# Causal attention with a rotated relative term: the query's rotation taken from its own product by four VectorE passes and moved a quarter of a step forward, and stage-start loads regrouped

## What is computed

```python
def _attn(xn, Wq, bq, Wk, bk, Wv, bv, Wo, bo, u):
    q = xn @ Wq.T + bq ; k = xn @ Wk.T + bk ; v = xn @ Wv.T + bv   # split into 16 heads of 8
    ...
    scores = q @ k.transpose
    rel = (q + u) @ r.transpose          # r: sin/cos position rows
    scores = (scores + _rel_shift(rel, S, S)) * HEAD_DIM ** (-0.5)
    ...                                   # causal mask, softmax, times v, out projection
```

## Time and profile before

| | us |
|---|---|
| median of three executions | 6445.04 |
| lowest, highest | 6442.2, 6449.46 |
| profiled execution | 6442.88 |
| its span | 6441.2 |
| granted TensorE clock, mean | 0.946 |
| busy: PE, DVE, ACT, POOL | 88%, 65%, 44%, 32% |

### The profile page before, as it was taken

One profiled execution on the slowest core, in us unless ns is written; L12 is line 12 of the kernel. 1 busy time (PEld: TensorE's weight loads), 2 busy tenths in 40 slices (PEclk: granted clock), 3 DMA queues, 4 the chain that ended last, 5 costly groups with the idle time before them and its releaser, 6 DMA issues. The chain is left out here.

```text
span 6441.2 us, 121160 instructions
## 1 busy us (share of the span) xinstructions
PE 5668.1 (88%) x38029; PEld 3515.6 (55%) x38029; DVE 4211.3 (65%) x9620; ACT 2847.4 (44%) x4602; POOL 2039.8 (32%) x2936
## 2 busy tenths in 40 slices
PE   8996999999996999879987998889988989875677
PEld 5663444444443777457754776467754556533464
DVE  6884666666664787367844786368745656577764
ACT  4553222222221555435553555445544645433344
POOL 6551000000002665156623665156620012251012
PEclk9998999999997999989998999899999999987799
DMA  4332332333334554055512554055510000000002
GB/s 132 108 104 89 97 97 96 99 95 96 96 98 108 145 150 127 6 135 149 149 49 74 147 149 112 7 154 151 150 27 4 0 3 0 5 4 0 0 2 60
DMA packets 526325, 526.98 MB, mean 82 GB/s; under 512 B 55698, under 2 KB 436705, under 8 KB 503780
## 3 DMA queue, kind: packets, MB, share of 16 engines
q1 hardware_dynamic: 517684, 517.90, 29.0%
q10 hardware_dynamic: 8320, 5.25, 0.3%
HBM read 337.88 MB, written 185.07 MB: 81 GB/s over the span
## 5 line engine op out<-in xcount | busy, mean ns | idle before, releaser
L351 DVE TENSOR_REDUCE a_mx<-a_unit 128x2 f32<-128x512 f32 (+1 forms) x1920 | 1295.1, 685 | 522.7 <-PE a_unit L537 506.6
L441 ACT ACTIVATE a_prob<-a_slot 128x1536 f32<-128x1536 f32 x640 | 929.1, 1452 | 575.6 <-PE a_slot L560 452.0
L535 PE MATMUL a_unit<-a_sk,a_sq 96*128 96x256 bf16 (+3 forms) x5120 | 758.7, 251 | 173.8 <-DMA a_sk<-a_kscratch 152.4
L1126 ACT ACTIVATE f_silu<-f_pG 128x512 f32<-128x512 f32 x528 | 315.0, 598 | 933.1 <-PE f_pG L1199 919.0
L537 PE MATMUL a_unit<-a_maskq,identb 128*128 128x256 bf16 (+1 forms) x1920 | 605.8, 316 | 0.0
L535 PEld LDWEIGHTS a_unit<-a_sk,a_sq 96*128 96x128 bf16 (+1 forms) x5120 | 373.0, 99 | 412.3 <-issue 168.5
L1068 DVE TENSOR_TENSOR f_gated<-f_spread,f_silu 128x512 f32<-128x512 f32 x512 | 354.6, 693 | 347.1 <-ACT f_silu L1126 307.0
L1178 PE MATMUL f_pO<-f_hidden,f_wd 128*128 128x512 f32 x1056 | 545.0, 598 | 13.5 <-DVE f_hidden L1070 13.3
L1199 PE MATMUL f_pG<-f_xnT,f_wg 128*128 128x512 f32 x1056 | 541.5, 594 | 0.0
L1203 PE MATMUL f_pU<-f_xnT,f_wu 128*128 128x512 f32 x1056 | 540.1, 593 | 0.0
L60 POOL TENSOR_SCALAR f_veps<-f_moments 128x4 f32<-128x4 f32 (+1 forms) x112 | 25.4, 227 | 1493.3 <-DVE f_moments L955 1031.0
(11 more groups left out here) (397 smaller groups left out, 11079.4 us busy)
## 6 DMA issues: line engine op xcount, KB each, us to landing
f_spread<-f_scratch SPq DMA_DIRECT2D x1024, 128.0 KB, 2.9
a_sq<-a_qscratch SPq DMA_DIRECT2D x128, 768.0 KB, 5.7
a_sk<-a_kscratch SPq DMA_DIRECT2D x160, 384.0 KB, 6.6
a_qscratch<-a_parts SPq DMA_DIRECT2D x288, 192.0 KB, 2.3
a_qscratch<-a_parts SPq DMA_DIRECT2D x288, 128.0 KB, 2.2
a_kscratch<-a_parts SPq DMA_DIRECT2D x160, 192.0 KB, 2.2
a_kscratch<-a_parts SPq DMA_DIRECT2D x160, 128.0 KB, 2.1
a_qscratch<-a_parts SPq DMA_DIRECT2D x288, 64.0 KB, 1.9
```

The costliest lines, as they stand in the source:

```text
L351: v.tensor_reduce(dst, src, op=ALU.max, axis=AX.X, negate=True).then_inc(red_done, 1)
L441: act.activation(prob[gr % 2][:, :], slot[:, :], ACT.Exp, scale=SCALE).then_inc(exp_done, 1)
L535: pe.matmul(bank[:, at * wide:(at + 1) * wide], q, sk[b][0:KM, gr * GH + h, 0:wide], start=(at == 0), stop=False)
L1126: act.activation(silu[c % 2][:, :], pG[c % 2][:, :], ACT.Silu).then_inc(silu_done, 1)
```

## The change

In `attention`:

- The weights `u12`, their load, the second product (L652) and its semaphore go. DVE forms `u1` and `u2` from the query/key product's own result, in which a head's features lie in another order, by four passes over 64 partitions each (`rotated`), from the halves of `ring[1]`'s query part and a rearranged table `turn`. Two passes come after the reduction of unit 4, two after that of unit 5; before, two passes of 128 partitions came after unit 7.
- DVE: the normalisation moves from after unit 4 to after unit 8, the division from after unit 5 to after unit 6.
- PE: the transposes of the normalised rows move to right behind scores(0), the query/key product to behind maxima(2), the value-projection product of n+1 comes after maxima(7), where that of n came after maxima(0).
- ACT: the copy-out of the transposed rows and the query/key product move ahead; the copy of the value projection follows the third group's exponentials, for n+1.
- POOL: `causal(2)` moves from ahead of the splitting chain to between the first subtraction and the second cast.

In the feed-forwards of the group and of l2: the weights, statistics and the first normalised tile live in a `FeedHead` that outlives the attention; the attention loads the weights, and in its last two steps makes the statistics of blocks 0 and 1 and normalises block 0. The performer only loads the weights. Nothing but PE and ACT waits for the weights, ACT runs one Gelu ahead, and g2's gain has a semaphore of its own, for which POOL waits a block later.

In `routed_experts`: the router's three arrays load first, on a semaphore of their own, for which DVE and PE wait; PE waits for the expert weights at its first expert product; ACT runs one Sigmoid ahead and doesn't wait.

```diff
@@ attention, POOL
                     causal(1)
-                    causal(2)
...
                         chain.link(g.tensor_copy(pt[:, :, 0, :], f32s[:, :, :]))
                         chain.link(g.tensor_tensor(rest[:, :, :], f32s[:, :, :], pt[:, :, 0, :], op=ALU.subtract))
+                    causal(2)
+                    if is_seq(n + 4):
+                        pt = parts[j % 2]
                         chain.link(g.tensor_copy(pt[:, :, 1, :], rest[:, :, :]))
...
+                    if head is not None and isinstance(n, int) and n >= SEQS - 1:
+                        blk = n - SEQS + 1
+                        g.wait_ge(head.stats_done, blk + 1)
+                        ln_rstd(g, chain, head.moments, head.veps, head.mhalf, head.rstd, eps, head.rstd_done, apart)
@@ attention, DVE
                     units(3, 5)
+                    def rotated(c, u):
+                        low = slice(c * D // 2, (c + 1) * D // 2)
+                        for o in range(2):
+                            ins = v.scalar_tensor_tensor(out=u[o * D // 2:(o + 1) * D // 2, :], in0=ring[1][low, 0:SEQ],
+                                                         scalar=b12s[low, c:c + 1], in1=turn[low, o, :],
+                                                         op0=ALU.add, op1=ALU.mult)
+                        return ins
...
+                    if rel and is_seq(n + 4):
+                        v.wait_ge(qk_taken, n + 5)
+                        if is_seq(n + 3):
+                            v.wait_ge(u_added, n + 4)
+                        rotated(0, u1)
                     units(5, 6)
+                    if rel and is_seq(n + 4):
+                        rotated(1, u2).then_inc(u_taken, 1)
+                    units(6, 7)
...
-                        v.scalar_tensor_tensor(out=u1[:, :], in0=ring[1][:, 0:SEQ], scalar=b12s[:, 0:1],
-                                               in1=turn[:, 0, :], op0=ALU.add, op1=ALU.mult)
-                        v.scalar_tensor_tensor(out=u2[:, :], in0=ring[1][:, SEQ:2 * SEQ], scalar=b12s[:, 1:2],
-                                               in1=turn[:, 1, :], op0=ALU.add, op1=ALU.mult).then_inc(u_taken, 1)
@@ attention, PE
                     scores(0)
-                    maxima(0)
-                    (value-projection product of n)
+                    (transposes of the normalised rows of n+4)
+                    maxima(0)
                     values(n - 1, (j + 1) % 2, 3)
                     maxima(1)
                     maxima(2)
+                    (query/key product of n+4)
...
                     maxima(7)
-                    if rel and is_seq(n + 4):
-                        pe.wait_ge(qk_taken, n + 5)
-                        for c in range(2):
-                            ins = pe.matmul(ring[1][:, c * SEQ:(c + 1) * SEQ], u12[:, c * D:(c + 1) * D], xnT[j % 4][:, :],
+                    if is_seq(n + 1):
+                        if is_seq(n + 4):
+                            pe.wait_ge(u_taken if rel else qk_taken, n + 5)
+                        (value-projection product of n+1)
@@ attention, DVE, end of the step
+                    if head is not None and once(n, SEQS - 1):
+                        v.drain()
+                        ln_stats(v, chain, rows(store, 0, BT), head.stats, head.moments, head.stats_done)
+                    if head is not None and once(n, SEQS):
+                        v.wait_ge(head.rstd_done, 1)
+                        ln_apply(v, rows(store, 0, BT), head.moments, head.rstd, head.xn).then_inc(head.xn_done, 1)
+                        v.drain()
+                        ln_stats(v, chain, rows(store, BT, BT), head.stats, head.moments, head.stats_done)
@@ feed_forward
             @block.gpsimd
-                g.wait_ge(w_in, W_IN)
+                    if gb is not None and once(n, 1):
+                        g.wait_ge(gain_in, 16)
             @block.scalar
-                act.wait_ge(w_in, W_IN)
+                act.activation(warm[:, :], core["ident"][:, 0:1], ACT.Gelu)
+                act.wait_ge(w_in, head.W_IN)
@@ routed_experts
+                for dst, src in ((wr[:, :], w["router"]), (bias[:, 0, :], w["bias"].partition_broadcast(P)),
+                                 (tri[:, :], core["tri"].partition_broadcast(P))):
+                    sp.dma_start(dst, src).then_inc(router_in, 16)
             @block.vector
-                v.wait_ge(w_in, W_IN)
+                v.wait_ge(router_in, ROUTER_IN)
             @block.tensor
-                pe.wait_ge(w_in, W_IN)
+                pe.wait_ge(router_in, ROUTER_IN)
...
+                        if once(n, 0):
+                            pe.wait_ge(w_in, W_IN)
```

More of the change, by code:

```diff
@@ L156, with attention @@
 KPART = [0, 1, 2, 0, 1, 0]
-def attention(nc, core, tag, store, eps, w, kept, layer=None, arriving=None):
+def attention(nc, core, tag, store, eps, w, kept, layer=None, arriving=None, head=None, head_w=None):
     rel = kept.rel
@@ L245, in _ @@
                     arriving.others(sp)
+                if head is not None:
+                    head.load(sp, head_w, layer)
                 def step(i, j):
@@ L493, in step @@
                     exps(2)
+                    if once(n, -1):
+                        act.wait_ge(kept.filled, 1)
+                    if is_seq(n + 1):
+                        act.wait_ge(v_pe, n + 2)
+                        if is_seq(n - 1):
+                            act.wait_ge(pv_done, n * GROUPS)
+                        hot = vaug[(j + 1) % 2][:, :, :, :].rearrange("p t (r f j) e -> p (t r) f j e", f=2, j=GH)
+                        got = ring[1][:, 0:SEQ].rearrange("p (a f j e) -> p a f j e", f=2, j=GH, e=HD)
+                        for f in range(2):
+                            ins = act.activation(hot[:, :, f, :, 16 * f:16 * f + HD], got[:, :, f, :, :], ACT.Copy)
+                        ins.then_inc(v_taken, 1)
                     if is_seq(n - 1):
@@ L589, in step @@
                     scores(0)
-                    maxima(0)
-                    if is_seq(n):
-                        if is_seq(n + 3):
-                            pe.wait_ge(u_taken if rel else qk_taken, n + 4)
-                        elif is_seq(n - 1):
-                            pe.wait_ge(v_taken, n)
-                        xb = xnT[j % 4]
-                        for t in range(QT):
-                            ins = pe.matmul(ring[1][:, t * D:(t + 1) * D], xb[:, t * P:(t + 1) * P], wq[:, 2 * D:3 * D],
-                                            start=True, stop=True)
-                        ins.then_inc(v_pe, 1)
-                    values(n - 1, (j + 1) % 2, 3)
-                    maxima(1)
                     if is_seq(n + 4):
@@ L611, in step @@
                         ins.then_inc(t_pe, 1)
+                    maxima(0)
+                    values(n - 1, (j + 1) % 2, 3)
+                    maxima(1)
                     maxima(2)
+                    if is_seq(n + 4):
+                        if once(n, -4):
+                            pe.wait_ge(w_qk, W_QK)
+                        pe.wait_ge(xnT_done, n + 5)
+                        for c in range(2):
+                            ins = pe.matmul(ring[1][:, c * SEQ:(c + 1) * SEQ], wq[:, c * D:(c + 1) * D], xnT[j % 4][:, :],
+                                            start=True, stop=True)
+                        ins.then_inc(qk_pe, 1)
                     if is_seq(n + 1):
@@ L742, in step @@
                 def step(n, b):
+                    if isinstance(n, int) and n < head.begun:
+                        return
                     if within(n + 2):
@@ L833, in _ @@
                 deep(pe, step)
+        for s in head.held.sems:
+            nc.gpsimd.sem_clear(s)
         k.clear()
@@ L1519, in _ @@
                     sp.dma_start(omega[h * HD:(h + 1) * HD, h * M:(h + 1) * M], w["omega"]).then_inc(w_in, 16)
+                head.load(sp, head_w)
             @block.gpsimd
```

152 lines of the change are left out of this document (75 added, 77 removed).

## The result

| | before | changed |
|---|---|---|
| median, us | 6446.61 (4 runs, 6442.2 to 6449.46) | 6563.24 (4 runs, 6553.9 to 6574.52) |
| profiled span | 6441.2 | 6562.3 |
| granted clock, mean | 0.946 | 0.945 |
| busy: PE, DVE, ACT, POOL | 88, 65, 44, 32% | 86, 66, 43, 31% |

The ratio of the runs is 1.0182, with a 95% interval of 1.0165 to 1.02: the change costs 117 us. The forecast was slower by 55 us (6500, range 6425 to 6600). The direction and the mechanism held; the size came out at twice the forecast, and one term of the sum carries most of that.

The account below looks back on a forecast made before the run. PE, busy 88%, was taken to bound the kernel, waiting mainly for the read-back of the split keys. The terms 52 − 8 − 2 + 44 − 15 − 13 − 4 − 2 = +52 gave 6500 us, range 6425 to 6600.

Parts of the forecast that it names:

- the stage starts: Earlier loads and statistics at the feed-forward and router stages: f0 −15, f1 −13, and −4 for a gain awaited late.
- a0: The first attention, without a rotation, its step set by DVE and PE together: −2 us, bounds −6 and +3.
- the steady step: Relative attention: rotation ends at 9.3 to 9.4, select at 14.5, step 16.6 us against 16.1; +52 us over 26 × 4.
- The clock: PE's granted clock falls behind the new wait on POOL's select in one step of four: +44 us.
- the clock holds: Rival: no clock falls behind PE's new wait in the attentions, so 6456 us; chance 0.13.
- a fall in every step: Rival: PE's clock falls behind the new wait in each of 104 steps, +177, so 6633 us; chance 0.08.
- The ramps: The ramp in at the start of the relative attention layers: −2 us, bounds −8 and +8.
- The last steps: A layer's last steps, without rotation, save the product and have no new wait: about 2 us a layer, −8.
- f0: Routed-experts stage: with the router's small arrays loaded first, DVE's first pass starts at 546 instead of 560.72: −15 us.
- f1: The layer group's feed-forward: loads made during attention remove a 3.6 us wait, less 0.3 for a table load; −13 in four layers.
- the rotation arrives in time: Rival: rotation done by about 7.2 us, select ready when PE comes, step about 15.0, 6285 us; wholly or partly, chance 0.18.
- The rival of DVE and POOL disturbing each other: Rotation passes and normalisation beside POOL's chain lengthen it by about 0.3 us a step: +31, 6531 us; chance 0.06.

Follow-up runs that it names:

- e1: The changed kernel with causal(2) put back ahead of POOL's splitting chain; 6344.7 us, ratio 0.9847 to the kernel before.
- e3: The changed kernel with two rotation passes over 128 partitions in place of four over 64; 6396.5 us, ratio 0.9928 to the kernel before.

## Why the prediction was right and wrong

Right: that the change makes it slower, and by what. The wait on POOL's select in every step (26 a layer), the end of the waits on `a_sk`, the loop of one step and its path are as forecast, and both directions of the edit confirm it (218 us less when undone, 557 more when done alone). The select stands 2.04 us before the next step, as read from the earlier trace rows; the removed product, the stage starts (−26 as a whole, forecast −32 without a0) and the place of the clock falls held too.

Wrong: the size of the steady step. The step that failed is "9.3 to 9.4" for the end of the rotation, and after it "14.5" for the select. Measured from 2940.11: 10.03 and 15.26.

| us | forecast | measured | off |
|---|---|---|---|
| PE ends unit 4 | 6.4 | 6.70 | +0.3 |
| from there to the rotation's end | 2.95 | 3.33 | +0.4 |
| add, cast, subtraction, select | 5.15 | 5.23 | +0.1 |
| select to next step | 2.09 | 2.10 | 0 |
| step | 16.6 | 17.36 | +0.76 |

The first row: I took the query/key product at the 0.86 of the removed one. Moved ahead it takes 1.05 (2943.02 to 2944.07). It starts on time, 0.06 after ACT's copy of the transposed rows, its input, is done (2942.96), where that copy used to be long done; that this is the reason for the 0.19 is likely, but no run shows it. The second: I took each pass at the 0.40 by which two passes over 128 partitions followed each other. The four over 64 took 0.96 and 0.99 a pair, with about 0.1 around them. The bounds were 0.20 and 0.48, and I chose by the nearer row; the high end was the right one. (The step of the earlier trace rows begins at 2403.88 in the trace, not at 2403.4 as I had it; no term hangs on that.) The 0.76 times 104 is +79, where the profiled execution is 69 above the sum; the other terms were off as well, and mostly cancelled each other, which is luck:

- The clock: falls in 12 steps of 104, not in one of four; 18 to 23 us, forecast 44. The rival "the clock holds" was nearer than "a fall in every step". Waits of 1.75 to 1.8 us were followed by falls in some steps, and filling them removed all; with 1.5 us in each step there was none. The rule of the Trainium skill ("TensorE: Matmul & The Clock Gate", section on HAM oscillation), by which only idle gaps well above these lower the clock, doesn't hold here; the measurement decides.
- The ramps: from the attention's start to its first output product 401 us in four layers against 384, +17, forecast −2. The steps of the ramp contain the same loop; I had counted 26 steps and forgotten those before. With the select in front this stretch took 378.
- The last steps: −14, forecast −8. a0: nothing (forecast −2). f0 −12.1 for −15, since its first pass started at 547.7 and not 546. f1 −16 for −13. The performer +3.9, forecast nothing.
- PE's own way: I had PE at the values of group 2 at 12.1, with a wait of 2.3. It came at 13.6 and waited 1.75. The short waits on DVE, above all for the longer passes, were not in the sum (with two passes it came at 12.6). They stay under the loop in the changed kernel, but they are part of why e1 runs at 15.5 and not at the 15.2 expected of it.

The rival "the rotation arrives in time" was the right idea of what the loop hangs on: e3's 1.2 us earlier rotation gave 167 us. The rival of DVE and POOL disturbing each other has no part in the loop: L332 took 1.64 as before, and the reductions 0.69. But the disturbance itself is in the traces, on DVE's side. Before, DVE's cast of the maxima stood beside POOL's second subtraction; in the changed kernel POOL is idle there. Two rows of before and one of the changed kernel:

```profile
2879.95 1.65 POOL L331 TENSOR_TENSOR a_parts<-a_rest,a_parts 128x768 bf16<-128x768 f32 x1
2880.32 1.31 DVE L376 CAST a_mparts<-a_mx 128x32 bf16<-128x32 f32 x1
...
2942.25 0.17 DVE L386 CAST a_mparts<-a_mx 128x32 bf16<-128x32 f32 x1
```

The cast ends at 2881.63, 0.03 after the subtraction. In the second layer it took 0.17 to 1.43 before, 0.66 in the median, and all 26 ended 0.03 to 0.06 after the end of a POOL instruction. In the changed kernel it takes 0.17 every time, and PE's wait for the cast and the subtraction behind it (L377 in the earlier trace rows) is gone. In return the normalisation, now beside L332, takes 1.44 to 1.52 for its pair, where it took 0.91 to 1.24. The reductions and the rotation's passes keep their length: 0.66 to 0.69 and 0.67 to 0.69 a reduction, 0.48 and 0.47 to 0.49 a pass.

## What to carry to other kernels

Follow a moved instruction on its in-order queue: the work that now stands ahead of it becomes its input, and if the engine waiting for it also feeds that work, the loop closes inside one step, and every microsecond in it is paid in full. When work is put on such a loop, take the dearer bound of its cost, and count the steps of the ramp. Shorter engine time (0.86 us of PE a step) bought nothing until the order of another engine's queue was right; then the same code was 1.5% faster than before, 0.4% of it from the stage starts. Which of the attention's other edits earns the rest no run takes apart.

## What the runs showed that was not expected

- Five added matmuls in a wait made the kernel 23 us faster, since TensorE's granted clock no longer fell to 1.2 GHz behind it.
- A pass of DVE over 64 partitions costs no less than one over 128: 0.96 to 0.99 for two of 256 columns, so 0.48 to 0.49 each, where the passes over 128 took 0.48 and 0.47.
- Four consecutive DVE passes in the old place cost twice what their length on the transfers' loop says (+90 instead of +45): PE, with two PSUM banks for the maxima, waited for DVE in each step, and the granted clock was lower. How the +45 that came on top divides between the two is open.
- A 128x32 cast on DVE ended only when POOL's instruction beside it did: 0.17 us alone, up to 1.43 beside one.
- An early division of 0.8 us on DVE removed PE's wait of 0.26 and brought one of 0.78 in each step.
